# A decoder layer on one core: the lower-threshold compare of the feed-forward weights moves from VectorE to GpSimd

## The chip, the core and the metric

The kernel runs on one core of a Trainium2 chip. Its five engines (TensorE, VectorE, ScalarE, GpSimd and SyncE, which here only issues DMAs) each work through their own list of instructions in order and meet through semaphores. The profile calls them PE (with PEld for weight loads), DVE, ACT, POOL and SP. The metric is the device time of one execution in microseconds; the kernel before takes 1132.5 us (median of 3 runs, 1131.54 to 1132.69).

## The reference

One decoder layer over x of shape (4, 512, 512), float32, in three parts, each with a residual:

```
x = x + attention(layernorm(x))                        # 16 heads, rotary, causal
x = x + ssm(ctx, gate = layernorm(x))                  # convolution, selective scan over 16 states, silu gate
x = x + bitlinear(gelu(bitlinear(layernorm(x), w_fc)), w_proj)

def ternarize_weights(w):
    gamma = jnp.mean(jnp.abs(w))
    return jnp.sign(jnp.round(w / (gamma + EPS))) * gamma
```

Both feed-forward matrices (2048 x 512 and 512 x 2048) are made ternary before use: a weight above half of gamma becomes +1, one below minus half becomes -1, all others 0. This is (w > thr) - (w < -thr) with thr = (gamma + 1e-6) / 2, and gamma is multiplied in later.

## The kernel before, in words

The four batches are worked through as a pipeline in which attention, the state-space scan and the feed-forward tiles of different batches overlap. The work is cut into named items. A planner (`plan()`) walks a table of due times (`schedule()`, with the constants of `WEIGHT`), the needs and assumed durations of each item (`follows()`), and writes one ordered list per engine, `ORDER["pe"]`, `ORDER["act"]`, `ORDER["dve"]`, `ORDER["pool"]`, `ORDER["sp"]`. It also decides the PSUM bank of each item, and how many dummy transposes (L1599) TensorE does while it stands by. The program of an engine is its list, item by item.

The items that matter here, with the lines of the profile:

- `dbu` (GpSimd, L1263) makes the scan's inputs in the ring `hb`; `exp` (ScalarE, L1394) makes its factors in PSUM; `scan` (VectorE, L1812, in the tail L1820) runs over `hb`; `ht` (TensorE L1725, VectorE L1834) turns the states and adds them up in `y_acc`. The factors of one scan are made only when the scan before it is through. In the last batch a piece is half as long (128x512).
- `s`, `e`, `t`, `pv`, `rz` are attention: row maxima on VectorE (L1905, L1909), exponentials on ScalarE (L1505), transposes, the product with v, the reciprocal of the sums (L1917). `wo` (TensorE L1737, VectorE L1932) is the output projection. `ln2a`, `ln2b` are the norm in front of the gate: statistics on VectorE, one power on GpSimd (L1317), one small operation on VectorE (L1947). `gate` is a silu on ScalarE (L1536), `gt` its product (VectorE L1956), `xadd` the residual on GpSimd (L1306).
- `fwload`, `wsum`, `wtot`, `tern` treat the feed-forward weights, matrix `w` = 0 (`raw_fc`) and 1 (`raw_pr`), in four parts of 128x2048 each: load, sum of absolute values on ScalarE (L1576, it writes its unused output to `low`), total over partitions and the thresholds `thr` and `nthr` on VectorE (L1963 to L1968), and then the ternary values.
- `tern` in the kernel before is two VectorE instructions for each part: L1977 writes `low` = (w < nthr) in bf16, L1979 writes (w > thr) - low over the same weights, in the form that TensorE reads (`t_fc`, `t_pr`). There is one `low` buffer, shared by all parts and by `wsum`. The semaphore `tern_done` counts both instructions.
- `xa`, `xc`, `xt`, `fc`, `hstat`, `hn`, `hscale`, `hq`, `ht_ffn`, `proj` are the 16 feed-forward tiles. `xc` is a subtraction and a maximum on VectorE (L2004, L2006), then a scaling on GpSimd (L1340).

Of the kernel before, what the change touches and what calls it, by code (L numbers as in the profile page):

```python
# [437 lines left out]
def follows(item):  # L438
# [157 lines left out]
        yield "dve", 1.2, [pe(*item)]  # L596
    elif kind == "tern":
        w, n = a
        yield "dve", 3.7, [dve("wtot", w)]
    elif kind == "fxload":  # L600
        t, = a
        yield "sp", 1.6, [sp("x2store", *divmod(t, LT)), dve("proj", t - XF) if t >= XF else pe("pv", SLOTS // 2 - 1)]
# [187 lines left out]
def layer_kernel(nc, t_in, out):  # L790
    sems = {}
    with ExitStack() as ctx:
# [185 lines left out]
        fw_in = [[sem(f"fw_in{w}{c}") for c in range(4)] for w in range(2)]  # L978
        wsum_ready = sem("wsum_ready")
        gam_ready = sem("gam_ready")  # L980
        tern_done = sem("tern_done")
        xf_in = [sem(f"xf_in{i}") for i in range(XF)]
        fx_var = sem("fx_var")
# [258 lines left out]
        def _(pool):  # L1242
# [11 lines left out]
            for kind, *a in ORDER["pool"]:  # L1254
# [64 lines left out]
                elif kind == "xa":  # L1319
# [12 lines left out]
                    own.done(nc.gpsimd.tensor_tensor(f[:, 3:4], f[:, 5:6], neg_half[:, 0:1], ALU.pow))  # L1332
                    own.settle()
                    nc.gpsimd.tensor_scalar(f[:, 7:8], f[:, 2:3], f[:, 3:4], None, ALU.mult).then_inc(fx_gain, 1)
                elif kind == "xc":

                    t, = a
# [27 lines left out]
        def _(act):  # L1365
# [7 lines left out]
            for kind, *a in ORDER["act"]:  # L1373
# [182 lines left out]
                elif kind == "fc":  # L1556
                    t, n = a
                    act.wait_ge(fc_full, 4 * t + n + 1)
                    act.wait_ge(fx_scale, t + 1)
                    if t >= 2:  # L1560
                        act.wait_ge(tr_full, TURN["ht_ffn", t - 2, 3] + 1)
                    elif t == 1:
                        act.wait_ge(xadd_done, LT * (B - 1))
                    nc.scalar.activation(h_sb[:, t % 2, 512 * n:512 * n + 512], bank(kind, t, n), ACT.Gelu,
                                         scale=fx[:, t % 4, 12:13]).then_inc(gelu_done, 1)
                elif kind == "wsum":

                    w, n = a
                    c = PARTS[w][n]
                    act.wait_ge(fw_in[w][c], 16)  # L1570
                    i = 4 * w + n
                    if i:
                        act.wait_ge(wsum_ready, i)
                    if w:
                        act.wait_ge(tern_done, 8)
                    nc.scalar.activation(low[:], raw[w][:, c, :], ACT.Abs, accum_out=w_sum[:, w, c:c + 1])\  # L1576
                        .then_inc(wsum_ready, 1)
                elif kind == "hn":

                    t, h = a  # L1580
                    act.wait_ge(fh_var, t + 1)
                    half = h_sb[:, t % 2, FF // 2 * h:FF // 2 * (h + 1)]
                    nc.scalar.activation(half, half, ACT.Identity, bias=fh[:, t % 4, 0:1], scale=-1.0).then_inc(hn_done, 1)
# [3 lines left out]
        def _(pe):  # L1587
# [13 lines left out]
            for kind, *a in ORDER["pe"]:  # L1601
# [174 lines left out]
                elif kind == "fc":  # L1776

                    t, n = a
                    pe.wait_ge(tr_free, TURN["xt", t] + 1)
                    pe.wait_ge(tern_done, 8)  # L1780
                    for d in range(KD):
                        for m, part in enumerate((xq_hi, xq_lo)):
                            mm = nc.tensor.matmul(bank(kind, t, n), part[:, t % 2, d, :], t_fc[:, d, 512 * n:512 * n + 512],  # L1783
# [1 line left out]
                    mm.then_inc(fc_full, 1)  # L1785
                elif kind == "proj":
                    t, = a
                    pe.wait_ge(tern_done, 16)
                    pe.wait_ge(tr_free, TURN["ht_ffn", t, 3] + 1)
                    for k in range(FT):  # L1790
                        for m, part in enumerate((hq_hi, hq_lo)):
# [6 lines left out]
        def _(dve):  # L1798
# [5 lines left out]
            for kind, *a in ORDER["dve"]:  # L1804
# [153 lines left out]
                elif kind == "wtot":  # L1958
# [6 lines left out]
                    v.tensor_scalar(g, g, 1.0 / (DM * FF), None, ALU.mult).then_inc(gam_ready, 1)  # L1965
                    dve.wait_ge(gam_ready, w + 1)
                    own.done(v.tensor_scalar(thr[:, w:w + 1], g, EPS_Q, 0.5, ALU.add, ALU.mult))
                    own.done(v.tensor_scalar(nthr[:, w:w + 1], g, EPS_Q, -0.5, ALU.add, ALU.mult))  # L1968
                    own.settle()
                elif kind == "tern":  # L1970

                    w, n = a
                    c, n = PARTS[w][n], 4 * w + n
                    dst = (t_fc[:, c, :], t_pr[:, 4 * c:4 * c + 4, :].rearrange("p a n -> p (a n)"))[w]
                    if n:
                        dve.wait_ge(tern_done, 2 * n)
                    v.tensor_scalar(low[:], raw[w][:, c, :], nthr[:, w:w + 1], None, ALU.is_lt).then_inc(tern_done, 1)  # L1977
                    dve.wait_ge(tern_done, 2 * n + 1)
                    v.scalar_tensor_tensor(out=dst, in0=raw[w][:, c, :], scalar=thr[:, w:w + 1], in1=low[:],  # L1979
                                           op0=ALU.is_gt, op1=ALU.subtract).then_inc(tern_done, 1)  # L1980
                elif kind == "xa":
# [147 lines left out]
```

## Time and profile before

| | |
|---|---|
| median of 3 runs | 1132.5 us (1131.54 to 1132.69) |
| the profiled execution | 1132.71 us, its span 1130.8 us |
| TensorE busy | 1003.4 us (89%) |
| VectorE busy | 958.6 us (85%) |
| ScalarE busy | 794.0 us (70%) |
| GpSimd busy | 630.2 us (56%) |
| mean granted TensorE clock | 0.961 of full speed |

The span runs from the first instruction to the last one that the profiler recorded; 1.9 us of the execution lie around it. Busy time is the time in which an engine had an instruction under way. As the stages have different limits, what a change in one of them is worth is read from that stretch of the span.

### The profile page before, as it was taken

Reading aid. Unit: us, or ns where it says so; the run is one execution under the profiler, and the core shown is the slowest. Engines: PE = TensorE matmul, PEld = TensorE weight load, DVE = VectorE, ACT = ScalarE, POOL = GpSimd, SP = SyncE. Lnnn points to the kernel's source line nnn. Section 1 sums busy time; section 2 is a strip of 40 time slices with the busy share of each in tenths; the row PEclk is TensorE's granted clock in tenths of the full one; section 3 lists DMA queues with packets and bytes.
Section 4 is the critical chain, followed back from the end, with each engine's and each line's share of the span. In section 5 each row is a group of like instructions: output and inputs, shape, how many; then the busy total and the mean of one; then the engine's idle time right before and its main releaser. Section 6 shows DMA issues by size and latency. Waiting matters only on the chain.

```text
span 1130.8 us, 19021 instructions
## 1 busy us (share of the span) xinstructions
PE 1003.4 (89%) x6054; PEld 762.8 (67%) x6054; DVE 958.6 (85%) x1351; ACT 794.0 (70%) x1533; POOL 630.2 (56%) x509
## 2 busy tenths in 40 slices
PE   6988998899988999898999986797788987999998
PEld 5555776566855567765558765676676776778887
DVE  5788679778698987988996889989999999998764
ACT  4854866667588776489867688955989888874342
POOL 1458468346336787526657853467766565653510
PEclk9999998999998999999999988799899999999999
DMA  4324546256445354333366371340111010100000
GB/s 158 113 85 140 160 136 184 64 150 196 129 117 152 128 162 145 127 115 112 112 186 190 106 237 50 110 171 10 52 38 37 30 52 29 24 15 20 19 19 19
DMA packets 59360, 115.91 MB, mean 103 GB/s; under 512 B 8880, under 2 KB 13232, under 8 KB 58240
## 3 DMA queue, kind: packets, MB, share of 16 engines
q1 hardware_dynamic: 59264, 114.70, 32.7%
q8 instruction: 51, 0.84, 0.3%
q14 instruction: 45, 0.37, 0.1%
HBM read 90.42 MB, written 24.25 MB: 101 GB/s over the span
## 4 chain that ended last, share of the span: by engine, by line
PE 54%; DVE 23%; issue 10%; ACT 8%; POOL 3%; DMA 1%; SPq 0%; DVEq 0%; ACTq 0%; POOLq 0%
PE ps L1656 8%; PE ps L1792 7%; PE ps L1725 7%; DVE hb L1812 6%; PE ps L1783 5%; PE ps L1737 5%; PE ps L1669 5%; PE ps L1699 4%; DVE y_acc L1834 4%; PE ps L1711 3%; DVE hb L1820 2%; PE ps L1680 2%; PE ps L1599 2%; DVE m_col L1909 2%; PE ps L1774 2%
## 5 line engine op out<-in xcount | busy, mean ns | idle before, releaser
L1263 POOL TENSOR_TENSOR hb<-du,b_bc 128x1024 f32<-128x1024 f32 (+1 forms) x160 | 312.1, 1972 | 147.0 <-PE ps L1725 141.6
L1812 DVE TENSOR_TENSOR_SCAN hb<-ps,hb 128x1024 f32<-128x1024 f32 (+1 forms) x128 | 257.6, 2014 | 21.7 <-ACT ps L1394 12.3
L1394 ACT ACTIVATE ps<-delta,a_neg 128x511 f32<-128x511 f32 (+2 forms) x320 | 180.5, 600 | 93.3 <-DVE hb L1812 78.9
L1834 DVE SCALAR_TENSOR_TENSOR y_acc<-ps,ct,y_acc 128x512 f32<-128x512 f32 x256 | 180.9, 740 | 29.7 <-PE ps L1725 29.0
L1725 PE MATMUL ps<-ident,hb 128*128 128x128 f32 x1088 | 155.4, 286 | 55.6 <-DVE hb L1812 28.6
L1725 PEld LDWEIGHTS ps<-ident,hb 128*128 128x128 f32 x1088 | 127.5, 146 | 87.3 <-issue 36.9
L1505 ACT ACTIVATE p_q<-ps,m_col 128x512 f32<-128x512 f32 (+3 forms) x256 | 131.5, 533 | 15.7 <-DVE m_col L1909 14.0
L1656 PE MATMUL ps<-xn_t,w_ring 128*128 128x512 f32 x256 | 118.3, 605 | 2.9 <-DVE hl L1890 2.9
L1699 PE MATMUL ps<-ident,p_q 128*128 128x128 f32 x640 | 93.9, 296 | 18.0 <-ACT p_q L1505 12.6
L1783 PE MATMUL ps<-t_fc,xq_hi 128*128 128x512 f32 x256 | 106.4, 415 | 2.6 <-DVE hq_lo L2026 1.2
L1521 ACT ACTIVATE p_t<-ps 128x512 f32<-128x512 f32 x160 | 86.0, 604 | 27.0 <-PE ps L1699 26.7
L1792 PE MATMUL ps<-t_pr,hq_hi 128*128 128x512 f32 x256 | 101.5, 396 | 0.6 <-DVE hq_lo L2026 0.6
L1783 PE MATMUL ps<-t_fc,xq_lo 128*128 128x512 f32 x256 | 102.0, 398 | 0.0
L1792 PE MATMUL ps<-t_pr,hq_lo 128*128 128x512 f32 x256 | 101.1, 395 | 0.0
L1699 PEld LDWEIGHTS ps<-ident,p_q 128*128 128x128 f32 x640 | 78.7, 152 | 32.5 <-ACT p_q L1505 17.3
L1909 DVE TENSOR_REDUCE m_col<-ps 128x1 f32<-128x512 f32 (+2 forms) x192 | 88.0, 501 | 10.6 <-PE ps L1684 8.0
L1656 PEld LDWEIGHTS ps<-xn_t,w_ring 128*128 128x128 f32 x256 | 47.4, 194 | 55.2 <-issue 49.6
L1680 PE MATMUL ps<-k_st,q_st 128*128 128x512 f32 (+3 forms) x256 | 74.8, 372 | 11.1 <-DVE y_acc L1834 6.1
L1599 PE MATMUL ps<-ident 128*128 128x128 f32 x498 | 68.6, 288 | 8.7 <-DMA small<-in_small 6.2
L1294 POOL TENSOR_TENSOR hl<-hl 128x512 f32<-128x512 f32 x16 | 20.4, 1274 | 97.7 <-DVE hl L1897 97.7
L1599 PEld LDWEIGHTS ps<-ident 128*128 128x128 f32 x498 | 60.4, 149 | 14.0 <-DMA small<-in_small 6.2
L1375 ACT ACT_TABLE_LOAD x47 | 60.3, 1283 | 0.8
(159 smaller groups left out, 2016.6 us busy)
## 6 DMA issues: line engine op xcount, KB each, us to landing
w_ring<-in_w_attn SPq DMA_DIRECT2D x32, 512.0 KB, 3.6
qk_d<-hl SPq DMA_DIRECT2D x64, 256.0 KB
q_st<-qk_d SPq DMA_DIRECT2D x128, 128.0 KB, 2.8
b_bc<-bc_d SPq DMA_DIRECT2D x48, 256.0 KB, 3.7
k_st<-qk_d SPq DMA_DIRECT2D x64, 128.0 KB, 2.7
k_st<-qk_d SPq DMA_DIRECT2D x128, 64.0 KB, 2.3
x_in<-in_x SPq DMA_DIRECT2D x16, 256.0 KB, 2.8
raw_fc<-in_w_fc SPq DMA_DIRECT2D x4, 1024.0 KB, 8.5
```

What stands on the lines that cost most here:

```text
L1263: nc.gpsimd.tensor_tensor(piece_of(e, hi, lo).rearrange("p (a n) -> p a n", a=2), du[b % 2][:, 2 * h:2 * h + 2, lo:hi], b_bc[:, i % BC_RIN ...
L1394: ins = nc.scalar.activation(factors(j, hi, lo)[:, (hi - lo) * m + start:(hi - lo) * (m + 1)], delta[b % 2][:, et, lo + start:hi], ACT.Exp ...
L1505: ins = nc.scalar.activation(p_q[:, h, Q_AT[i]:Q_AT[i] + w], src[:, col:col + w], ACT.Exp, bias=m_col[:, i, h:h + 1], accum_out=z_sum[:, b ...
L1599: nc.tensor.transpose(bank(*item)[:, 0:P], ident[:], ident[:])
L1656: mm = nc.tensor.matmul(bank(kind, *a), w_ring[:, c % 2, d, P * half:P * half + P], xn_t[:, d, :], start=(d == 0), stop=(d == KD - 1))
L1699: mm = nc.tensor.transpose(dst[:, at:at + P], p_q[:, h, Q_AT[i] + P * jt:Q_AT[i] + P * jt + P], ident[:])
L1725: mm = nc.tensor.transpose(bank(kind, *a)[:, P * et:P * et + P], piece_of(2 * r + et // 2, hi, lo)[:, at:at + P], ident[:])
L1783: mm = nc.tensor.matmul(bank(kind, t, n), part[:, t % 2, d, :], t_fc[:, d, 512 * n:512 * n + 512], start=(d == 0 and m == 0), stop=(d == K ...
L1792: mm = nc.tensor.matmul(bank(kind, t), part[:, k, :], t_pr[:, k, :], start=(k == 0 and m == 0), stop=(k == FT - 1 and m == 1))
L1812: v.tensor_tensor_scan(h, d, h, 0.0, ALU.mult, ALU.add).then_inc(scan_done, 1)
L1834: v.scalar_tensor_tensor(out=y, in0=bank(kind, r, tb), scalar=ct[:, b % 2, tb, n:n + 1], in1=y, op0=ALU.mult, op1=ALU.add).then_inc(y_free ...
L1909: ins = v.tensor_reduce(m_col[:, i, h:h + 1], src[:, col:col + P * (i + 1)], AX.X, ALU.max, negate=True)
```

## The change

The first instruction of `tern` moves from VectorE to GpSimd. A new semaphore `thr_ready` tells GpSimd that the thresholds of a matrix stand, `low_ready` tells VectorE that a part's compare is through, and `tern_done` now counts only VectorE's instruction, so that all waits on it halve. GpSimd's compare of a part waits for VectorE's combination of the part before, since there is one `low`. The planner is told of a GpSimd share of 4.7 and a VectorE share of 2.5 in place of one VectorE share of 3.7.

```diff
     elif kind == "tern":
         w, n = a
-        yield "dve", 3.7, [dve("wtot", w)]
+        yield "pool", 4.7, [dve("wtot", w)] + ([dve("tern", *divmod(4 * w + n - 1, 4))] if w or n else [])
+        yield "dve", 2.5, [pool(*item)]
...
+                elif kind == "tern":
+
+                    w, n = a
+                    c, n = PARTS[w][n], 4 * w + n
+                    pool.wait_ge(thr_ready, w + 1)
+                    if n:
+                        pool.wait_ge(tern_done, n)
+                    nc.gpsimd.tensor_scalar(low[:], raw[w][:, c, :], nthr[:, w:w + 1], None, ALU.is_lt).then_inc(low_ready, 1)
...
                     if w:
-                        act.wait_ge(tern_done, 8)
+                        act.wait_ge(tern_done, 4)
...
                     own.done(v.tensor_scalar(thr[:, w:w + 1], g, EPS_Q, 0.5, ALU.add, ALU.mult))
-                    own.done(v.tensor_scalar(nthr[:, w:w + 1], g, EPS_Q, -0.5, ALU.add, ALU.mult))
+                    v.tensor_scalar(nthr[:, w:w + 1], g, EPS_Q, -0.5, ALU.add, ALU.mult).then_inc(thr_ready, 1)
...
-                    if n:
-                        dve.wait_ge(tern_done, 2 * n)
-                    v.tensor_scalar(low[:], raw[w][:, c, :], nthr[:, w:w + 1], None, ALU.is_lt).then_inc(tern_done, 1)
-                    dve.wait_ge(tern_done, 2 * n + 1)
+                    dve.wait_ge(low_ready, n + 1)
                     v.scalar_tensor_tensor(out=dst, in0=raw[w][:, c, :], scalar=thr[:, w:w + 1], in1=low[:],
                                            op0=ALU.is_gt, op1=ALU.subtract).then_inc(tern_done, 1)
```

Since the planner reads these shares, the lists of all engines differ from the first feed-forward total on (the `wtot` of matrix 0, near 682 us of the trace); ahead of it they are the same. In the lists the lines of the changed kernel are 3 to 11 higher on GpSimd and VectorE. ScalarE's list holds 97 table loads in place of 100.

GpSimd around the parts of matrix 0 (`hb` are the scan's inputs, `du` those of the next batch). Before:

```order
L1263 TENSOR_TENSOR hb<-du_98,b_bc 128x1024 x11
L1288 TENSOR_TENSOR du_95<-delta_96,du_95 128x512 x4
L1263 TENSOR_TENSOR hb<-du_95,b_bc 128x512 x8
```

After:

```order
L1266 TENSOR_TENSOR hb<-du_98,b_bc 128x1024 x5
L1345 TENSOR_SCALAR low<-raw_fc,nthr 128x2048
L1266 TENSOR_TENSOR hb<-du_98,b_bc 128x1024 x2
L1345 TENSOR_SCALAR low<-raw_fc,nthr 128x2048 x2
L1266 TENSOR_TENSOR hb<-du_98,b_bc 128x1024 x2
L1345 TENSOR_SCALAR low<-raw_fc,nthr 128x2048
L1266 TENSOR_TENSOR hb<-du_98,b_bc 128x1024 x2
```

The first compare stands ahead of the pair of scan inputs for which GpSimd was free before, and the second and third stand together ahead of the next pair.

VectorE in the same place (`gam`, `thr`, `nthr` are the total and the thresholds, the 128x1024 operations on `hb` the scans). Before:

```order
L1968 TENSOR_SCALAR nthr<-gam 128x1
L1977 TENSOR_SCALAR low<-raw_fc,nthr 128x2048
L1979 SCALAR_TENSOR_TENSOR t_fc<-raw_fc,thr,low 128x2048
L1812 SCALAR_TENSOR_TENSOR hb<-ps,hb 128x1024
L1834 SCALAR_TENSOR_TENSOR y_acc<-ps,ct,y_acc 128x512
L1917 RECIPROCAL z_sum<-z_sum 128x16
```

After:

```order
L1979 TENSOR_SCALAR nthr<-gam 128x1
L1845 SCALAR_TENSOR_TENSOR y_acc<-ps,ct,y_acc 128x512
L1823 SCALAR_TENSOR_TENSOR hb<-ps,hb 128x1024
L1928 RECIPROCAL z_sum<-z_sum 128x16
L1823 SCALAR_TENSOR_TENSOR hb<-ps,hb 128x1024
L1987 SCALAR_TENSOR_TENSOR t_fc<-raw_fc,thr,low 128x2048
```

Two scans now stand ahead of the first combination.

GpSimd behind the output projection `wo`, with the third and fourth compare of matrix 1 (`xq` is the scaling of a feed-forward tile, `rstd_72` the power that the norm in front of the gate waits for, `xr` the residual). Before:

```order
L1340 TENSOR_SCALAR xq<-xq,fx 128x512
L1345 TENSOR_SCALAR fx<-fx,gam 128x1
L1317 TENSOR_TENSOR rstd_72<-ve_71,neg_half 128x4
```

After:

```order
L1351 TENSOR_SCALAR xq<-xq,fx 128x512
L1356 TENSOR_SCALAR fx<-fx,gam 128x1
L1266 TENSOR_TENSOR hb<-du_95,b_bc 128x512
L1345 TENSOR_SCALAR low<-raw_pr,nthr 128x2048
L1320 TENSOR_TENSOR rstd_72<-ve_71,neg_half 128x4
L1309 TENSOR_TENSOR xr<-xr,y_acc 128x512 x4
L1345 TENSOR_SCALAR low<-raw_pr,nthr 128x2048
```

The power now stands behind a scan input and a compare.

## Rows read from the trace of the kernel before

**Rows 1.** The page, part 4: the chain by engine, share of the span.

```profile
PE 54%; DVE 23%; issue 10%; ACT 8%; POOL 3%; DMA 1%; SPq 0%; DVEq 0%; ACTq 0%; POOLq 0%
```

**Rows 2.** Windows: stretch, length, busy us (count) per engine, PE clock, DMA share, GB/s.

```profile
680.00:700.00 20.00, 13.30 (x124) 9.66 (x122) 19.82 (x20) 16.60 (x31) 5.70 (x2) 0.83 0.18 56
700.00:720.00 20.00, 13.38 (x73) 10.67 (x74) 19.73 (x23) 18.59 (x37) 6.73 (x3) 0.78 0.02 7
...
780.00:800.00 20.00, 13.65 (x78) 11.48 (x76) 19.78 (x23) 19.73 (x25) 16.02 (x13) 0.91 0.03 8
...
980.00:1000.00 20.00, 17.58 (x90) 14.21 (x88) 19.79 (x34) 15.54 (x23) 12.50 (x17) 1.00 0.14 33
...
1020.00:1040.00 20.00, 20.00 (x109) 16.86 (x107) 18.42 (x32) 7.65 (x12) 7.11 (x12) 1.00 0.07 27
```

**Rows 3.** Timeline of VectorE, matrix 0: start, duration, instruction, idle time before it.

```profile
682.60 2.48 DVE L1977 TENSOR_SCALAR low<-raw_fc,nthr 128x2048 bf16<-128x2048 f32 x1
685.11 4.36 DVE L1979 SCALAR_TENSOR_TENSOR t_fc<-raw_fc,thr,low 128x2048 fp32r<-128x2048 f32 x1
689.39 2.28 DVE L1812 TENSOR_TENSOR_SCAN hb<-ps,hb 128x1024 f32<-128x1024 f32 x1
...
692.39 1.19 DVE L1977 TENSOR_SCALAR low<-raw_fc,nthr 128x2048 bf16<-128x2048 f32 x1
693.62 2.35 DVE L1979 SCALAR_TENSOR_TENSOR t_fc<-raw_fc,thr,low 128x2048 fp32r<-128x2048 f32 x1
...
724.45 1.28 DVE L1977 TENSOR_SCALAR low<-raw_fc,nthr 128x2048 bf16<-128x2048 f32 x1
```

**Rows 4.** Timeline of GpSimd beside it.

```profile
681.62 5.70 POOL L1263 TENSOR_TENSOR hb<-du,b_bc 128x1024 f32<-128x1024 f32 x2 [2.77 <-PE ps L1725]
704.33 4.69 POOL L1263 TENSOR_TENSOR hb<-du,b_bc 128x1024 f32<-128x1024 f32 x2 [17.01 <-PE ps L1725]
```

**Rows 5.** Lines by form: line, engine, operation, count, busy us, mean ns, idle before.

```profile
L1263 POOL TENSOR_TENSOR hb<-du,b_bc 128x512 f32<-128x512 f32 x64 | 85.4, 1357 | 30.7 <-PE ps L1725 30.7
...
L1340 POOL TENSOR_SCALAR xq<-xq,fx 128x512 f32<-128x512 f32 x16 | 32.4, 2026 | 12.8 <-DVE fx L2008 11.9
...
L1251 POOL TENSOR_SCALAR_AFFINE_SELECT ident_r<-xn_t 128x128 fp32r<-128x128 f32 x1 | 0.3, 292 | 0.3 <-POOL xn_t L1248 0.3
...
L1246 POOL MEMSET neg_half<- 128x4 f32 x1 | 0.1, 101 | 0.0
```

**Rows 6.** Timeline of ScalarE: factors of a scan, a sum of weights; the page's table loads.

```profile
691.78 1.30 ACT L1394 ACTIVATE ps<-delta,a_neg 128x511 f32<-128x511 f32 x2 [1.58 <-DVE hb L1812]
732.57 1.91 ACT L1576 ACTIVATE low<-raw_pr 128x2048 bf16<-128x2048 f32 x1
...
L1375 ACT ACT_TABLE_LOAD x47 | 60.3, 1283 | 0.8
```

**Rows 7.** Timeline of TensorE: the output projection.

```profile
755.86 13.98 PE L1737 MATMUL ps<-w_ring,o_t 128*128 128x256 f32 x64
```

**Rows 8.** Timeline of VectorE, matrix 1.

```profile
758.17 1.27 DVE L1977 TENSOR_SCALAR low<-raw_pr,nthr 128x2048 bf16<-128x2048 f32 x1
...
767.73 2.33 DVE L1812 TENSOR_TENSOR_SCAN hb<-ps,hb 128x512 f32<-128x512 f32 x2
...
779.48 0.16 DVE L1947 SCALAR_TENSOR_TENSOR nmr<-mv,rstd 128x4 f32<-128x4 f32 x1 [0.41 <-POOL rstd L1317]
...
782.44 0.67 DVE L1990 BATCH_NORM_STATS2 st_x<-xf 128x6 f32<-128x512 f32 x1
...
783.24 1.26 DVE L1977 TENSOR_SCALAR low<-raw_pr,nthr 128x2048 bf16<-128x2048 f32 x1
...
786.80 0.68 DVE L1956 TENSOR_TENSOR y_acc<-ps,y_acc 128x512 f32<-128x512 f32 x1
...
791.10 1.47 DVE L1977 TENSOR_SCALAR low<-raw_pr,nthr 128x2048 bf16<-128x2048 f32 x1
```

**Rows 9.** Timeline of GpSimd behind the output projection.

```profile
778.41 1.04 POOL L1317 TENSOR_TENSOR rstd<-ve,neg_half 128x4 f32<-128x4 f32 x1
```

More of the change, by code:

```diff
@@ L980, in layer_kernel @@
         gam_ready = sem("gam_ready")
+        thr_ready = sem("thr_ready")
+        low_ready = sem("low_ready")
         tern_done = sem("tern_done")
@@ L1779, in _ @@
                     pe.wait_ge(tr_free, TURN["xt", t] + 1)
-                    pe.wait_ge(tern_done, 8)
+                    pe.wait_ge(tern_done, 4)
                     for d in range(KD):
@@ L1787, in _ @@
                     t, = a
-                    pe.wait_ge(tern_done, 16)
+                    pe.wait_ge(tern_done, 8)
                     pe.wait_ge(tr_free, TURN["ht_ffn", t, 3] + 1)
```

## The prediction, made before the changed kernel ran

> **What bounds the kernel now.** I read the page first, then the windows of the span, then the timelines of VectorE and GpSimd around the ternary conversion. The page gives TensorE 54% of the chain, VectorE 23% [rows 1]; that is an average, and the conversion lies in a stretch that looks otherwise. From 680 to 720 us VectorE is busy 19.8 and 19.7 of 20 us, TensorE only 13.3 and 13.4, GpSimd 5.7 and 6.7 [rows 2]: VectorE sets the pace, and GpSimd has time. From 756 to 770 us TensorE runs the output projection without a gap, 13.98 us [rows 7], and VectorE's work beside it costs nothing. From 780 us VectorE is full again (19.78 of 20, still 19.79 at 980 to 1000), and from 1020 us TensorE is (20.00 of 20) [rows 2], up to the end. So a microsecond taken from VectorE at 680 to 728 us or behind 780 us should come out at the end, and one taken at 756 to 770 us should not.
>
> **The price of the compare on GpSimd.** The trace has no one-operation compare of this engine, so I bound it. A select over 128 columns took 292 ns, a fill of 4 columns 101 ns [rows 5]: less such a start it is 1.5 ns a column, which for 2048 columns makes 3.2 us. A two-input multiply took 4.69 us for two of 1024 columns, so 4.7 us for 2048 [rows 4]. A tensor_scalar with two operations took 2026 ns for 512 columns, so up to 8.1 us for 2048 [rows 5]. The compare does one operation on one input. I take 4.0 us, the middle of the two one-operation rows, and keep 3.2 and 8.1 as ends. The page "GPSIMD Engine Reference" of the Trainium skill, section "Engine selection", says that one-input operations run at roughly line rate; at its 1.2 GHz that is an estimate of 1.7 us, below my lower end, and by it the sum would be that of the first rival. No row here shows such a rate: the two-operation row is far above it.
>
> **Stretch 1, matrix 0 (682 to 728 us).** Four compares leave VectorE: 2.48, 1.19 and, for the third like the fourth, 1.28, together 6.2 us [rows 3]. What comes back:
> - The second scan behind the thresholds now stands ahead of the first combination. Its factors are made only after the first scan, 1.30 us [rows 6], a gap that the second compare and combination filled before. VectorE has only the reciprocal for it: +1.3.
> - A combination that meets a GpSimd multiply is stretched: 4.36 us beside the pair at 681.62, 2.35 alone [rows 3, 4], 2.0 more. The first combination meets a pair in both kernels. The third is new in this: GpSimd starts the next pair as soon as its third compare is through. Bounds 0 and 2.0; I take +1.0.
> - The waits for `low_ready`. GpSimd runs the first compare from 682.6 to 686.6; VectorE comes to the combination at about 689.3 (682.5 and an operation of 0.7, two scans of 2.2 [rows 3], 1.5 between them). The combination of 4.36 ends at 693.7 and releases the second compare, to 697.7; VectorE has a scan and four operations of 0.65 first, to 698.4. The third runs from 700.9 to 704.9, VectorE has a scan and seven small operations, to about 707.4. So no wait at 4.0 us; from 4.7 us on it begins. The scan inputs that are pushed back (from 681.6 to 686.6) still land before their scan at 694.
> Sum -3.9 us.
>
> **Stretch 2 (728 to 756 us).** ScalarE's second sum of matrix 1, 1.91 us and its readout [rows 6], moves from a place where ScalarE had time to one between scan factors, ahead of the total that stands before the output projection. Bounds 0 and 2.1; I take +1.0. The projection begins 2.9 us earlier.
>
> **Stretch 3 (756 to 770 us).** Two compares leave VectorE (the first 1.27 us [rows 8], the second like it), both beside the projection [rows 7]: 0. GpSimd's two compares must fit there with VectorE's combinations between them: 756 + 4.0 + 2.35, a little VectorE work, then 4.0 + 2.35 again ends at about 769, with the projection's end at 769.8. From a compare of 4.4 us on this decides, and each further microsecond costs two.
>
> **Stretch 4 (770 to 800 us).** Two compares leave VectorE: 1.26 + 1.47 = -2.7 [rows 8]. By the new order two scans (2.33 us) come from ahead of the projection's end to behind it, +2.3, and two gate products (0.68 each) and a statistics step (0.67) go the other way into covered time, -2.0 [rows 8]. The power for the norm stands behind a scan input and a compare: GpSimd is through with the second scaling at about 778.4 [rows 9], then about 1.3 (a scan input, from the 1357 ns of [rows 5]) + 4.0 + 1.04 give 784.7, where VectorE comes to it at about 782.2; before, it waited 0.41 [rows 8]. In VectorE's list the scans and everything else queue behind that small instruction, and ScalarE's factors and TensorE's turns behind the scans: +2.5. The fourth compare waits for the residual additions and ends at 793.7, VectorE is there at 792.9: +0.8. The third combination meets the residual additions, which read two inputs: bounds 0 and 2.0, +1.0. Sum +1.9 us.
>
> **Behind 800 us** the same work stands in another order on a full VectorE and then a full TensorE: 0. ScalarE's list holds three table loads less, 1.28 us each [rows 6], 3.8 us; they lie beside the full VectorE, so I count 0 and keep 3.8 for the better end.
>
> **Sum.** -3.9 + 1.0 + 0 + 1.9 = -1.0 us. The profiled execution took 1132.71 us (span 1130.8 and 1.9 around it), which is the median of the runs, 1132.5, within 0.02%. 1132.7 - 1.0 = 1131.7 us. That is inside 0.2% (2.3 us), about what a measurement of this kernel can tell from no change.
>
> **On the port.** Rows show a combination of 4.36 us against 2.35, and VectorE's compare of 2.48 against about 1.28, each beside the same GpSimd pair, which itself took 5.70 in place of 4.69 [rows 3, 4]. The page "SBUF — State Buffer" of the Trainium skill, section "Who interferes with whom", says why: a VectorE instruction with two SBUF inputs, or in a mode that takes both ports, shares a port pair with GpSimd, and whoever starts second is held for the whole instruction of the other. The trace agrees with a hold of one instruction. That rule speaks against the change, since it puts eight long GpSimd reads beside VectorE; what it gives is the third rival.
>
> **Rivals.**
> 1. *The saving comes through.* The compare takes 3.2 us and no combination meets a multiply. Then stretch 1 gives -4.9, stretch 2 nothing, stretch 4 -2.7 + 2.3 - 2.0 + 1.7 = -0.7: -5.6 us, 1127.1 us, and down to 1123.3 if the table loads count too. For it: GpSimd stands idle 17.01 us in front of one pair [rows 4]. Against: the norm's power is behind a compare whatever it costs.
> 2. *The compare takes the two-operation rate (slower).* At 7.6 us, a little under the 8.1 of [rows 5], VectorE waits for `low` 1.0, 3.1 and 0.9 us in stretch 1, +5.0. In stretch 3 both compares and combinations end at 776.2 in place of 770: +6.2, on the way of the first feed-forward tile, because VectorE's last drain of the projection stands behind the second combination. In stretch 4 the power and the fourth compare come 3.6 us later each, +7.2. Together 18.4 more than the forecast: 1150.1 us. It decides from about 4.7 us on. For it: the only long tensor_scalar of GpSimd has this rate. Against: that one does two operations.
> 3. *VectorE is held (slower).* The compare is short, but the fourth stands beside VectorE's subtraction for the third tile, which is of the kind that was stretched from 1.28 to 2.48, and is held up to 4.0 us, with up to 1.0 more for the third combination. That makes 1134.7 to 1136.7 (3.0 to 5.0 more), say 1135.7 us. Against: it takes an overlap that depends on a microsecond.
> That the change does nothing can be left out: the compares leave VectorE for certain.
>
> **How the numbers follow.** Chances: forecast 0.32 (of it 0.26 within 0.2%, 0.04 faster, 0.02 slower), rival 1 0.31 (0.29 faster, 0.02 within), rival 2 0.21 (all slower), rival 3 0.16 (0.13 slower, 0.03 within). That makes faster 0.33, within 0.31, slower 0.36. The likeliest is the forecast, 1131.7 us; its own range by the bounds of the two collisions and of the sum's move is 1128.7 to 1134.8. As cases of both signs hold much of the chance, the whole range is 1125 to 1147, which leaves out the far end of rival 1 and something over half of rival 2.
>
> **What would show it.** GpSimd's compare in the profile after: 3 to 5 us bears the forecast or rival 1, 7 to 8 us rival 2. VectorE's combination at 2.35 us in all but two or three of eight; four or more near 4.4 us, or a VectorE tensor_scalar of 128x512 above 2 us, bear rival 3. The small norm operation should wait for the power some 2.5 us, the first combinations not at all for `low`. The projection should begin near 753 us. If the compare is short and VectorE has no new waits, yet the end comes late, then the order behind 800 us, which I counted as nothing, was not nothing, and the prediction is wrong there.

## The result and the profile after

The changed kernel takes 1151.37 us (median of 4 runs, 1147.39 to 1153.46), the kernel before 1132.60 us beside it: ratio 1.0162, 95% interval [1.0147, 1.0177], so 18.4 us slower. The forecast was 1131.7 us with a range up to 1147. The profiled execution took 1153.46 us (span 1151.7). Left out of every figure below are three executions of over 3300 us (3376.56 in e1, 3336.59 in e4, 4696.50 in e7; in the two that were profiled TensorE was busy for the whole span), so that e1 was profiled once more, as e1b.

The page, part 4, of the changed kernel, against [rows 1]:

```profile
PE 48%; DVE 21%; issue 12%; ACT 10%; POOL 8%; DMA 1%; SPq 0%; DVEq 0%; ACTq 0%; POOLq 0%
```

GpSimd's share of the chain went from 3% to 8%: it is now waited for. The groups of GpSimd's instructions on `low` (count, shortest, median and longest in ns, first and last start):

```profile
L1345 POOL TENSOR_SCALAR low<-raw_fc,nthr x4: 5432/5437/5457, 682.9 to 715.2; 128x2048 bf16<-128x2048 f32 x4
L1345 POOL TENSOR_SCALAR low<-raw_pr,nthr x4: 5443/5456/5462, 755.4 to 800.6; 128x2048 bf16<-128x2048 f32 x4
```

A compare is 5.44 us where I had taken 4.0 (and where the estimate of 1.7 us that the prediction sets beside it is three times too short). The windows, against [rows 2], columns as there:

```profile
680.00:700.00 20.00, 13.46 (x115) 10.08 (x117) 16.09 (x17) 18.76 (x36) 17.05 (x4) 0.83 0.18 55
700.00:720.00 20.00, 15.11 (x103) 11.06 (x95) 18.41 (x19) 10.85 (x26) 17.45 (x5) 0.82 0.12 32
780.00:800.00 20.00, 12.80 (x64) 10.61 (x64) 13.84 (x15) 5.84 (x11) 17.05 (x11) 0.84 0.17 60
...
1020.00:1040.00 20.00, 17.25 (x90) 14.17 (x91) 19.79 (x34) 16.25 (x24) 11.09 (x17) 1.00 0.00 1
```

At 780 to 800 us VectorE is busy 13.84 us where it was 19.78: it stands still there, in the stretch in which it had set the pace. VectorE's timeline of the changed kernel at matrix 0, against [rows 3]:

```profile
689.42 3.47 DVE L1987 SCALAR_TENSOR_TENSOR t_fc<-raw_fc,thr,low 128x2048 fp32r<-128x2048 f32 x1
...
700.55 2.35 DVE L1987 SCALAR_TENSOR_TENSOR t_fc<-raw_fc,thr,low 128x2048 fp32r<-128x2048 f32 x1 [2.14 <-POOL low L1345]
```

GpSimd's and then VectorE's timeline at matrix 1, against [rows 8, 9]:

```profile
755.43 5.46 POOL L1345 TENSOR_SCALAR low<-raw_pr,nthr 128x2048 bf16<-128x2048 f32 x1
760.87 0.22 POOL L1327 TENSOR_SCALAR fx<-fx 128x1 f32<-128x1 f32 x1
761.17 2.53 POOL L1329 TENSOR_TENSOR fx<-fx,neg_half 128x1 f32<-128x1 f32 x1
...
765.47 5.46 POOL L1345 TENSOR_SCALAR low<-raw_pr,nthr 128x2048 bf16<-128x2048 f32 x1
...
785.65 5.45 POOL L1345 TENSOR_SCALAR low<-raw_pr,nthr 128x2048 bf16<-128x2048 f32 x1
791.06 1.04 POOL L1320 TENSOR_TENSOR rstd<-ve,neg_half 128x4 f32<-128x4 f32 x1
792.07 4.99 POOL L1309 TENSOR_TENSOR xr<-xr,y_acc 128x512 f32<-128x512 f32 x4
800.62 5.44 POOL L1345 TENSOR_SCALAR low<-raw_pr,nthr 128x2048 bf16<-128x2048 f32 x1 [3.57 <-DVE t_pr L1987]
```

```profile
760.93 2.35 DVE L1987 SCALAR_TENSOR_TENSOR t_pr<-raw_pr,thr,low 128x2048 fp32r<-128x2048 f32 x1 [1.72 <-POOL low L1345]
...
770.97 3.35 DVE L1987 SCALAR_TENSOR_TENSOR t_pr<-raw_pr,thr,low 128x2048 fp32r<-128x2048 f32 x1 [4.86 <-POOL low L1345]
774.24 0.68 DVE L1943 TENSOR_TENSOR xr_last<-ps,xr_last 128x512 f32<-128x512 f32 x1
...
792.14 4.93 DVE L1958 SCALAR_TENSOR_TENSOR nmr<-mv,rstd 128x4 f32<-128x4 f32 x1 [4.20 <-POOL rstd L1320]
...
801.03 5.31 DVE L2012 TENSOR_SCALAR xq<-xf,fx 128x512 f32<-128x512 f32 x1
```

VectorE comes to the second combination 4.86 us too early, and the last drain of the projection (774.24) stands behind it. It waits 4.20 us for the norm's power. The small product `nmr`, 0.16 us before, takes 4.93 us: it starts as GpSimd's four residual additions do and ends with them. In this text an instruction that starts beside one of GpSimd's, lasts much longer than elsewhere and ends just behind it is called held. A 128x512 subtraction, 0.48 us before, takes 5.31: it ends 0.28 us behind the fourth compare. TensorE's timeline, against [rows 7]:

```profile
754.79 13.98 PE L1748 MATMUL ps<-w_ring,o_t 128*128 128x256 f32 x64
781.89 1.11 PE L1785 MATMUL ps<-ident,xq 128*128 128x128 f32 x4 [9.85 <-POOL xq L1351]
808.55 1.94 PE L1736 MATMUL ps<-ident,hb 128*128 128x128 f32 x8 [13.53 <-DVE hb L1823]
```

TensorE waits 9.85 us in front of tile 0's first transposes, and later 13.53 us for the scan that stands behind the held subtraction on VectorE.

Five marks place the loss. The first is the first feed-forward total on VectorE (681.97 before), up to which every kernel here runs the same instructions; then the start of the projection (755.86), tile 0's first transposes (775.88), tile 0's hidden statistics on VectorE (801.39, the aggregate of 128x24) and the span (1130.8). In us against before, from one profiled execution each:

| kernel | first total | projection | transposes | statistics | span |
|---|---|---|---|---|---|
| changed | +0.3 | -1.1 | +6.0 | +16.4 | +20.9 |
| e1b: its lists, all work on VectorE | +1.5 | +2.4 | +2.9 | +5.9 | +9.6 |
| e2: only matrix 0 on GpSimd | +1.6 | -0.8 | -0.3 | +2.7 | +6.1 |
| e3: only matrix 1 on GpSimd | -2.0 | -1.1 | +6.0 | +12.5 | +16.1 |
| e10: e1, tail of before | -3.1 | -1.0 | -0.4 | +2.3 | +4.7 |
| e16: e1, lists of matrix 0 alone | +0.1 | +0.3 | +0.3 | +0.3 | +1.9 |
| e17: e1, lists of matrix 1 alone | -0.7 | -0.6 | +0.9 | +6.4 | +9.2 |
| e18: e1, three items put back | +1.4 | +4.3 | +6.4 | +10.3 | +13.1 |
| e14: compares half as long | +1.0 | -4.8 | -2.7 | -1.3 | +2.1 |
| e12: matrix 0 alone, planned so | -0.5 | -3.1 | -3.1 | -3.3 | -0.8 |
| e19: e12 and 22 empty matmuls | -0.6 | -3.2 | -3.2 | -3.4 | -2.4 |

What stands under "first total" is the execution's own and no work of the change, and has to be taken off the other columns: e1b and e10, alike up to tile 0's statistics, come to it 4.5 us apart, and once it is taken off they differ by 1.2 us at the projection and 1.0 at the statistics. One execution is no median even so (that of e3 lies 6 us under the median of its runs). The marks show where, and the medians and ratios below show how much.

### The profile page after: what moved, and what is told of

Read it like the earlier page. It is cut to its first block, busy times and chain, and to the rows that moved or that the text cites. A ratio compares the mean times of both kernels' runs of the same rounds, so it can differ in the third digit from the quotient of the medians.

```text
span 1151.7 us, 18999 instructions
## 1 busy us (share of the span) xinstructions
PE 1002.3 (87%) x6042; PEld 758.2 (66%) x6042; DVE 957.7 (83%) x1343; ACT 789.6 (69%) x1530; POOL 671.9 (58%) x517
## 4 chain that ended last, share of the span: by engine, by line
PE 48%; DVE 21%; issue 12%; ACT 10%; POOL 8%; DMA 1%; SPq 0%; DVEq 0%; ACTq 0%; POOLq 0%
PE ps L1667 8%; PE ps L1803 7%; PE ps L1736 6%; PE ps L1680 5%; DVE hb L1823 5%; PE ps L1710 4%; PE ps L1794 4%; PE ps L1748 3%; POOL hb L1266 3%; DVE y_acc L1845 3%; PE ps L1722 2%; ACT ps L1405 2%; DVE hb L1831 2%; DVE m_col L1920 2%; PE ps L1691 2%
## 5 line engine op out<-in xcount | busy, mean ns | idle before, releaser
L1266 POOL TENSOR_TENSOR hb<-du,b_bc 128x1024 f32<-128x1024 f32 (+1 forms) x160 | 316.2, 1994 | 124.6 <-PE ps L1736 119.5
L1736 PE MATMUL ps<-ident,hb 128*128 128x128 f32 x1088 | 158.4, 289 | 71.1 <-DVE hb L1823 41.9
L1691 PE MATMUL ps<-k_st,q_st 128*128 128x512 f32 (+3 forms) x256 | 72.6, 363 | 13.1 <-DVE y_acc L1845 7.6
L1610 PE MATMUL ps<-ident 128*128 128x128 f32 x486 | 66.2, 284 | 8.1 <-DMA small<-in_small 5.6
L1610 PEld LDWEIGHTS ps<-ident 128*128 128x128 f32 x486 | 57.5, 147 | 13.2 <-DMA small<-in_small 5.6
L1575 ACT ACTIVATE h_sb<-ps,fx 128x512 f32<-128x512 f32 x64 | 43.0, 685 | 26.8 <-PE ps L1794 26.4
```

What stands on the lines that cost most here:

```text
L1266: nc.gpsimd.tensor_tensor(piece_of(e, hi, lo).rearrange("p (a n) -> p a n", a=2), du[b % 2][:, 2 * h:2 * h + 2, lo:hi], b_bc[:, i % BC_RIN ...
L1610: nc.tensor.transpose(bank(*item)[:, 0:P], ident[:], ident[:])
L1736: mm = nc.tensor.transpose(bank(kind, *a)[:, P * et:P * et + P], piece_of(2 * r + et // 2, hi, lo)[:, at:at + P], ident[:])
```

## The experiments

Theory A: the loss is the length of the compares at matrix 1 and what they hold up. Rival B: the new lists lose by themselves.

**Lists, and each matrix apart.** e1 keeps the lists of the change, but VectorE does both instructions; e2 and e3 leave one matrix on GpSimd.

```diff
+ON_POOL = ()                     # e1; (0,) in e2, (1,) in e3
...
 GpSimd:   elif kind == "tern":
+    if w not in ON_POOL: continue
...
 VectorE:  elif kind == "tern":
+    if w not in ON_POOL:
+        v.tensor_scalar(low[:], raw[w][:, c, :], nthr[:, w:w + 1], None, ALU.is_lt).then_inc(low_ready, 1)
```

> All lists of the changed kernel, but VectorE does both instructions of every part, one after the other, and GpSimd none. Theory A (the price is GpSimd's compare of 5.44 us and what it blocks): about the time before, 1130 to 1138 us, since VectorE gets its 10 us of compares back and loses its waits. Rival B (the new order of the lists is what costs): at least 1145 us.

> Lists of the changed kernel, GpSimd compares matrix 0 only, VectorE does both instructions for matrix 1. Theory A: matrix 0 waited only 2.1 us for the compare in the changed kernel and had its compares of 6 us removed, so this is 1 to 4 us faster than the kernel with the same lists and no compare on GpSimd. Rival B: as that kernel, at least 1145 us.

> Lists of the changed kernel, GpSimd compares matrix 1 only. Theory A: nearly the whole loss is here (waits of 1.7 and 4.9 us for the compare, 4.2 for the norm's power, 4.8 and 4.8 us in which VectorE's small norm operation and its subtraction were held): 1146 to 1154 us. Rival B: as the kernel with the same lists and no compare on GpSimd, within 2 us.

Measured: e1 1140.10 us, ratio 1.0061 [1.0044, 1.0078], between what A and what B gave; e2 1138.40, 1.0041 [1.0026, 1.0055]; e3 1154.60, 1.0178 [1.0149, 1.0206]. With the changed kernel that is a square of two by two. By the ratios the lists cost 7 us with no work moved, GpSimd's compares of matrix 0 give 2 us back (inside the intervals) and those of matrix 1 cost 13. The three add up to the whole. A is right for matrix 1, B for the rest; my forecast had neither. VectorE's timeline of e3, where the changed kernel had 4.93 and 5.31:

```profile
792.15 1.24 DVE L1961 SCALAR_TENSOR_TENSOR nmr<-mv,rstd 128x4 f32<-128x4 f32 x1 [4.22 <-POOL rstd L1321]
...
797.35 0.82 DVE L2020 TENSOR_SCALAR xq<-xf,fx 128x512 f32<-128x512 f32 x1
...
804.74 3.34 DVE L1995 SCALAR_TENSOR_TENSOR t_pr<-raw_pr,thr,low 128x2048 fp32r<-128x2048 f32 x1 [3.27 <-POOL low L1348]
```

The long holds that A counted on are not there, and still this execution loses 13.6 us between projection and statistics, against 17.5 in the changed kernel. Of VectorE's waits it has one more, 3.27 us for the fourth compare. So the waits carry most of the loss at matrix 1, and the long holds some 4 us of it in the executions that have them.

**The lists of before.** e4 keeps them and only inserts the eight compares into GpSimd's list.

```diff
+ORDER["pool"].insert(ORDER["pool"].index(after) + 1, ("tern", w, n))
```

> Lists of the kernel before on all engines; GpSimd's eight compares are put into its list where it had time: two behind the scan inputs 91, one each behind 93 and 95, behind the first feed-forward scale of the second tile, behind 105, behind the norm's power, and behind the third tile's scaling. VectorE has only the combinations. Theory A: the norm's power comes in time, so it is cheaper than the changed kernel, but the compares of matrix 1 still do not fit beside the output projection and still hold VectorE: 1134 to 1146 us. Rival B: the removed compares come through, 1122 to 1130 us.

Measured: 1163.71 us, 1.0271 [1.0254, 1.0288], slower than either theory had it. VectorE's waits from 660 to 860 us (in total, times, longest):

```profile
DVE t_pr L1992 <- POOL low L1350: 21.3, 4, 7.1
DVE t_fc L1992 <- POOL low L1350: 19.2, 4, 9.3
```

All eight combinations wait. With the compares at these places in the lists of before, the kernel is 12 us slower by the ratios than with the new lists, which themselves cost 7 against before. Other places were not tried.

**What the holds cost.** e6 writes `nmr` as four one-input instructions of 128x1, e7 puts the norm's power ahead of GpSimd's third compare.

```diff
-v.scalar_tensor_tensor(out=nmr, ...)                 # 128x4, two inputs
+for i in range(4): v.tensor_scalar(nmr[:, i:i + 1], ...)
...
+_p.insert(_p.index(("tern", 1, 2)), ("ln2a", B - 1))     # e7, GpSimd's list
```

> The changed kernel, with one edit: the small norm operation on VectorE, one instruction of 128x4 with two tensors from SBUF that lasted 4.93 us beside four residual additions of GpSimd, is written as four of 128x1, each with one tensor and scalars. Theory D (it was held at the port by its second tensor): none of the four lasts over 0.3 us, and the kernel gains 2 to 5 us, 1146 to 1150 us. Rival (the record shows something else, a late semaphore or GpSimd's own load): they end as late as before and the time stays at 1151 us.

> The changed kernel, with the norm's power of the last batch put ahead of GpSimd's third compare of matrix 1. Theory A: VectorE's wait of 4.2 us for it goes, and the compare ends 1.0 us later; 3 to 6 us faster, 1145 to 1149 us. Rival (what is taken here comes back as a wait for the third or fourth compare, since VectorE comes to them earlier): less than 1.5 us.

Measured: e6 1148.19 us, 1.0132 [1.0115, 1.0149], 3.4 us better by the ratios than the change. VectorE's timeline of e6:

```profile
790.37 0.58 DVE L1959 TENSOR_SCALAR nmr<-mv,rstd 128x1 f32<-128x1 f32 x4 [4.22 <-POOL rstd L1320]
790.86 1.21 DVE L1823 TENSOR_TENSOR_SCAN hb<-ps,hb 128x512 f32<-128x512 f32 x1
791.99 5.44 DVE L1988 SCALAR_TENSOR_TENSOR t_pr<-raw_pr,thr,low 128x2048 fp32r<-128x2048 f32 x1
```

`nmr` is free, the scan too, and now the third combination, 2.32 us in the change, is held until the additions (790.29 to 795.29 here) are through and ends 2.1 us behind them. So the hold moved on to the next two-input instruction. e7: 1150.20 us, 1.0156 [1.0139, 1.0173]: no gain from putting the power first. That what it frees is waited for later was the rival's reading; the profile of e7 is of an execution of 4696.50 us and doesn't show it.

**The length.** e14 compares 1024 of the 2048 columns.

```diff
-nc.gpsimd.tensor_scalar(low[:], raw[w][:, c, :], nthr[...], None, ALU.is_lt)
+nc.gpsimd.tensor_scalar(low[:, :1024], raw[w][:, c, :1024], nthr[...], None, ALU.is_lt)
```

> The change with each GpSimd compare over 1024 of the 2048 columns; the other half of `low` is left as it stood, so half of the thresholding is not computed. The compare should take 2.7 to 2.8 us if its time goes by columns (5.44 at 2048). Theory A (13 us of the loss is the length of the compares at matrix 1, above all the two ahead of tile 0's transposes, plus the holds): with half the length 1139 to 1143 us, near e1's 1141.0, and less the 2.6 us of matrix 0 perhaps 1137. Rival H (the loss is the handover between the engines and VectorE's holds, not the length): above 1146 us.

Measured: 1134.73 us, 1.0014 [1.0001, 1.0027]. Groups of e14:

```profile
L1345 POOL TENSOR_SCALAR low<-raw_fc,nthr x4: 2843/2846/2867, 683.6 to 712.2; 128x1024 bf16<-128x1024 f32 x4
L1345 POOL TENSOR_SCALAR low<-raw_pr,nthr x4: 2848/2862/2862, 751.7 to 788.0; 128x1024 bf16<-128x1024 f32 x4
```

2.6 us less per compare brings 16.8 us (1.0162 less 1.0014, times 1132.6) of the 18.4 back. Lists and handovers are the same: what the change pays for hangs on the length, and rival H falls as a cost of its own. The waits go with it: VectorE waits 1.69 us for the norm's power and 0.71 in all for `low` of matrix 1, and in this profile `nmr` takes 1.24 us and the subtraction 0.85. It is 4 us under A's range, and 5 faster than e1 with the same lists. So the 7 us of the lists are their price with the work as it is in e1, and are no fixed charge.

**The planner's price.** e8 tells the planner 5.5 for a compare; e15 does half of each compare on either engine, all of it computed, with 2.8 and 3.1.

```diff
-yield "pool", 4.7, ...
+yield "pool", 5.5, ...          # e8; in e15 2.8, and VectorE 3.1 in place of 2.5
...
+v.tensor_scalar(low[:, 1024:], raw[w][:, c, 1024:], nthr[...], None, ALU.is_lt)   # e15, VectorE
```

> The change with one number altered: the planner counts 5.5 us for a compare on GpSimd in place of 4.7. The third compare of matrix 0 then stands one scan-input product later, and the tail is ordered anew. Theory A (the compare's real length costs 13 us at matrix 1, wherever the list puts it, since nothing can be moved under it): 1146 to 1152 us. Rival G (the planner merely had the wrong price and with the right one avoids the waits): 1133 to 1142 us.

> A version that the results point to: of each part GpSimd compares columns 0 to 1023 and VectorE columns 1024 to 2047 (0.63 us), then VectorE combines all 2048; the planner counts 2.8 us and 3.1 us. Everything is computed. By e14 a half compare takes GpSimd 2.7 us and is in time for VectorE. If the length was what cost the change its 18 us, and the lists do no harm, the four us that VectorE is spared show in part: 1128 to 1132 us. If an order made for new costs loses by itself as in e1: 1134 to 1141 us.

Measured: e8 1148.79 us, 1.0136 [1.0120, 1.0152]; e15 1138.20 us, 1.0036 [1.0022, 1.0050]. The right price saves 3 us (the two intervals touch) and not the change, as A said. The halves are slower than before too, as the second case had it: its tile 0 transposes wait 8.07 us for GpSimd's scaling, 2.99 before.

**Which lists.** e16 and e17 take the lists of one matrix each, with all work on VectorE. e1b is the profile of e1.

```diff
 elif kind == "tern":
+    if w in PLANNED:            # (0,) in e12, e16, e19; (1,) in e17
         yield "pool", ...       # 5.5 in e12, e16, e19; 4.7 in e17
         yield "dve", 2.5, ...
+    else:
+        yield "dve", 3.7, [dve("wtot", w)]
```

> The lists of e12 (only matrix 0 planned on GpSimd), but VectorE does both instructions of all eight parts and GpSimd none. Theory I (the new order around matrix 0 costs nothing, and GpSimd's compares give the little that e12 has): 1132 to 1134 us, and tile 0's statistics at 801 to 802 us. Rival J (this order by itself costs 2 to 3 us, which e12's compares pay for; the lists' loss of e1 lies partly here): 1135 to 1137 us.

> Only matrix 1 is planned on GpSimd (at 4.7 us, as in the change), and VectorE does both instructions of all eight parts. Theory K (the lists' 8 us of e1 lie in matrix 1's part and the tail that it reorders): 1138 to 1142 us. Rival J (they lie in matrix 0's part): 1132 to 1135 us.

> e1 once more for its profile. From e2 and e10: tile 0's statistics on VectorE (801.39 us before) at 804 to 806 us, the end 6 to 8 us late. If the lists' loss lies ahead (theory E): the statistics 5 us late or more; if behind (theory D): under 3 us late and 5 us lost after that.

Measured: e16 1134.10 us, 1.0002 [0.9991, 1.0012]; e17 1142.38, 1.0075 [1.0061, 1.0089]; e1b 1142.21 (one run). The lists' loss is matrix 1's alone. By the marks of e17, 7 us of it fall between the start of the projection and tile 0's statistics and 3 behind; by those of e1b, less its 1.5 at the first total, 0.9 ahead of the projection, 3.5 there and 3.7 behind.

**What in them.** e5 puts GpSimd's scalings of tiles 4 to 9 ahead of the scan's operands in e1. e10 follows the change's lists up to tile 0's statistics and those of before from there. e18 puts back matrix 1's total and scans 104 and 105.

```diff
 e10: lists[engine] = head of the change + [x for x in before[engine] if x not in head]
 e18: move("pe", [("wtot", 1)], ahead of ("ht", 54, 0)); move("dve", [("wtot", 1)], ahead of ("xa", 0))
      move("dve", [("scan", 104), ("scan", 105)], ahead of ("wo", 3, 1, 1))
```

> As the kernel with the changed lists and both instructions on VectorE (1141.0 us), but in GpSimd's list the scaling of the feed-forward tiles 4 to 9 stands ahead of the one, two or three scan inputs that the new order put before it, as in the kernel before. Theory C (the lists cost their 8 us because TensorE waits for that scaling, 9.0 us in five waits from 832 to 1004 us in the kernel with matrix 0 on GpSimd, none before): 4 to 7 us faster, 1134 to 1137 us. Rival (the 8 us are spread over the order of VectorE and ScalarE): less than 2 us, 1139 us or more.

> The lists of e1 again, with both instructions of every part on VectorE, but spliced: each engine follows the lists of the changed kernel up to tile 0's statistics (VectorE's `hstat` 0, near 815 us) and the lists of the kernel before from there on; banks and empty matmuls are worked out anew for the spliced lists. e1 lost 8.1 us to the lists. Theory D (the loss lies in the order behind 815 us, in tiles 0 to 9, as the starts of the output tiles suggest: 1.9 us early at tile 0 in e2, 6.1 us late at the end): with the tail of the kernel before nearly all comes back, 1131 to 1135 us. Rival E (the head lists leave the engines in a state, by what was pulled ahead or put off, from which the tail is late whatever its order): 1139 to 1142 us, as e1.

> e1 (lists of the change, all work on VectorE) with three items put back where the kernel before has them: the weight sum of matrix 1 ahead of the conversion statistics of tile 0 on VectorE and ahead of state turn 54 on TensorE, and scans 104 and 105 ahead of the last projection copy, so ahead of tile 0's first transposes. Theory L (tile 0's chain is late because VectorE, which has no idle time there, does this work first): 2.3 to 5 us come back, 1136 to 1139.5 us, and tile 0's statistics stand 2 to 5 us earlier than in e1b_look. Rival M (the place of these items does not matter, the loss is spread over many small swaps): 1140 to 1143 us.

Measured: e5 1145.13 us, 1.0105 [1.0090, 1.0120], 5 us worse than e1 by the ratios; the same edit on e2 (e9) gave 1141.42, 1.0075 [1.0059, 1.0091], 4 us worse. e10 1138.98, 1.0049 [1.0035, 1.0064]: 1.4 us better than e1, inside the intervals. e18 1142.47, 1.0085 [1.0069, 1.0102]: not better. Theories C (the scaling's place), D (the tail's order) and L (these three items) all fall as the main cause. Which swap in the lists of matrix 1 costs the 7 to 8.5 us stays open. For the stretch between projection and statistics the profiles show by what it comes. VectorE's timeline of e1b:

```profile
762.56 2.05 DVE L1993 TENSOR_SCALAR low<-raw_pr,nthr 128x2048 bf16<-128x2048 f32 x1
764.65 3.23 DVE L1995 SCALAR_TENSOR_TENSOR t_pr<-raw_pr,thr,low 128x2048 fp32r<-128x2048 f32 x1
...
798.19 3.26 DVE L1995 SCALAR_TENSOR_TENSOR t_pr<-raw_pr,thr,low 128x2048 fp32r<-128x2048 f32 x1
```

Before, these take 1.28, 2.35 and 2.35 us. Here each meets a scan-input multiply of GpSimd that is already under way; before, the multiplies beside the two combinations start 0.09 and 0.14 us behind them, and it is GpSimd that takes longer. In this stretch VectorE does the same work in both kernels. What its instructions last beyond the median of their form in the kernel before adds up to 5.2 us in e1b and to 0.2 before, and it is idle 1.3 us less: together 3.7 us, where the marks give 3.5. In e17 the two terms are +5.2 and +2.0 for 7.0 us (`nmr` alone waits 3.41 and takes 3.73 us), in e18 +7.4 and -0.5 for 6.0. This is read from one execution each and was not put to the test. The 3 to 4 us behind the statistics stay open.

**A version that is not slower.** e12 plans and runs matrix 0 alone on GpSimd; VectorE's list in it is that of before from 767 us of the trace on, not from 740 as the text below has it: a gate product and a few other items around the projection stand elsewhere. e19 adds empty matmuls ahead of one state turn.

```diff
+FILLS["ht", 60, 0] += 22        # e19
```

> The planner is told of matrix 0 alone that GpSimd compares (at 5.5 us, what the compare takes), and of matrix 1 that VectorE does both (3.7 us); the kernel does so. The lists differ from those before only up to the first output projections (near 740 us) and are the same word for word behind. Theory D: the 2.6 to 3.2 us that matrix 0 gave in e2 are kept and nothing is lost behind: 1129 to 1131 us, faster than before. Rival E (what the lists lost, they lost ahead of 800 us): 1136 to 1140 us, as e2. Rival F (matrix 0's gain is absorbed by what is late next, the gate transposes and matrix 1): 1132 to 1134 us.

> e12 with 22 empty matmuls ahead of state turn 60 on TensorE, where it stood idle for 3.0 us at 814 us before the granted clock fell to 0.56 and 0.58 in 816 to 824 us (1.00 in the kernel before). Theory N (the half clock takes what tile 0 had won): the clock stays at 1.00 there and the end comes 1 to 2 us earlier than e12's, 1130 to 1131 us. Rival O (the end is set by VectorE, which hardly notices the clock): no difference, 1131.5 to 1132.5 us. If the empty matmuls stand in the way of the scans' inputs instead: 1133 us or more.

Measured: e12 1132.09 us, 0.9992 [0.9981, 1.0003]; e19 1130.86 us, 0.9985 [0.9975, 0.9994]. e12 is what rival F gave, e19 what theory N gave. Windows of e12, of e19:

```profile
808.00:816.00 8.00, 6.27 (x32) 4.91 (x30) 7.79 (x15) 7.43 (x12) 3.91 (x7) 1.00 0.00 2
816.00:824.00 8.00, 6.73 (x23) 5.87 (x24) 7.84 (x11) 7.05 (x13) 6.06 (x8) 0.57 0.10 30
```

```profile
808.00:816.00 8.00, 8.00 (x50) 6.95 (x49) 7.79 (x15) 7.42 (x13) 4.07 (x7) 1.00 0.02 4
816.00:824.00 8.00, 6.66 (x40) 5.37 (x39) 8.00 (x11) 7.20 (x12) 6.30 (x8) 1.00 0.19 32
```

Counted from the first total, e12 is 2.8 us early at tile 0's statistics and 0.3 at the end. In it TensorE stood idle 3.0 us up to 817.27, and in the 8 us from 816 on the granted clock averages 0.57, near its lower level (1.2 in place of 2.4 GHz). The kernel before has 1.00 there, but 0.79 in the 8 us ahead of it. With the gap filled the clock stays at 1.00 in both stretches, and this execution is 1.8 us early at the end. By the ratios the empty matmuls are worth 0.8 us, inside the intervals of the two. e19 beats the kernel before by 1.7 us [0.7, 2.8], less than the 0.2% I had called measurable, though the interval excludes no change; the changed kernel it beats by 20.

## Why the prediction was wrong

*The price.* "I take 4.0 us": it is 5.44, between my ends. I averaged a start-corrected select and a two-input multiply. The nearest row by kind, the tensor_scalar [rows 5], would have missed by more the other way (8.1), so no row gave the price; the multiply (4.7) and the tensor_scalar hold it between them. By the two lengths, 5.44 and 2.85 us, a column costs 2.5 ns and the start 0.3 us. The trace before had none of this, but my text had the point from which the price decides, 4.4 to 4.7 us, only just above my value: a forecast so near its own threshold should have leaned to the other side of it.

*Stretch 1, -3.9.* Measured -1.4 at the projection, counted from the first total, where stretches 1 and 2 together were to give -2.9. The second combination waits 2.14 us for `low`, which I had at nothing and rival 2 at 3.1. The first combination met the pair as in the forecast, but takes 3.47 in place of 4.36; the collision of the third, +1.0, did not come (2.34). The sign held, and e2 and e12, with the same compares, come to -2.4 and -2.6: these two stretches were nearly right.

*Stretch 3, 0.* This is the step that failed most, that both compares fit beside the projection and cost nothing: +7.1 between projection and transposes, where rival 2 had +6.2 from a compare of 7.6. I had called VectorE's work there covered by the projection, and both were full: before, VectorE is busy 13.89 of the 14.00 us from 756 to 770, so that nothing longer than what left could pass unseen. I had placed the second compare right behind the first combination. In GpSimd's list tile 1's six factor instructions stand between them, 760.87 to 765.47, one of them a 0.56 us power that VectorE's combination stretches to 2.53. So the mechanism of rival 2 decided at a price of 5.44 already.

*Stretch 4, +1.9.* Measured +10.4 (from +6.0 to +16.4). The wait for the power was foreseen at 2.5 and is 4.2. The hold of the subtraction was rival 3's ("held up to 4.0"), and came to 4.83 us more than its own time. That of `nmr`, 4.77 us more, was in no case: I had looked for one of the third combination there (+1.0), which at 2.32 us was not held. I had read the port from one pair of instructions as a hold of one instruction. The page "SBUF — State Buffer" of the Trainium skill, section "Who interferes with whom", says that the one that comes first has the shared ports for its whole instruction while the other is blocked. The first combination agrees: it starts at 689.42 beside the first multiply of a pair and ends 2.15 us behind that one, and the pair takes 6.73 in place of 4.69 us, since the second multiply waits in its turn. `nmr` was held over four additions, so the measurement goes further. e6 shows that avoiding one hold moves it to the next candidate, and e3 that the loss is mostly there without the long ones.

*Behind 800 us, 0.* Wrong, as the last sentence of the prediction allowed for. The changed kernel loses 4.5 us behind tile 0's statistics. The lists cost 7 us with no work moved (e1) and 8.5 with matrix 1's alone (e17). More than half of that is ahead of 800 us, where I had priced the moved instructions one by one at +0.3 (+2.3 - 2.0) and not whom they would meet on GpSimd. In the square the terms are: lists +7 (forecast near 0), matrix 0's compares -2, matrix 1's +13 (forecast near 0).

*Rival 2* was the right mechanism with a chance of 0.21 and a time of 1150.1 us, 1.3 from the result. That nearness is luck in part: it had the compare 2 us too long and held the lists at nothing.

## What to carry to other kernels

Work is given to an idle engine only if each piece is short against the slack at its place, not against the engine's idle share: half the length took away 16.8 of 18.4 us lost, and the same work at a place with slack (matrix 0) gave 1 to 2 us by the ratios, each time inside the intervals. Price an unseen instruction by a range between the nearest rows on either side, and when the threshold lies within that range, let the forecast follow the worse side. Compare profiles from the last point up to which the kernels do the same, not from the start. Where a planner orders everything, run its new lists without the moved work first: that separates the cost of the order from that of the work (here 7 against 13 us, less the 2 that matrix 0 gives back).

## What was not expected of the hardware

- GpSimd's one-operation compare of 128x2048 f32 into bf16 takes 5.43 to 5.47 us, and 2.84 to 2.87 for 1024 columns. It hardly varies beside other work.
- A two-input VectorE instruction can be held over a whole run of back-to-back GpSimd two-input instructions: 4.93 us for a 128x4 product beside four additions of 4.99. It need not be: with the same start beside the same additions the product took 1.24 us in e3, to the end of the first. What decides between the two, no run here shows. In e18 a combination of 2.35 took 5.89 beside three scan-input multiplies:

```profile
799.97 3.77 POOL L1284 TENSOR_TENSOR hb<-du,b_bc 128x512 f32<-128x512 f32 x3
```

```profile
799.99 5.89 DVE L2012 SCALAR_TENSOR_TENSOR t_pr<-raw_pr,thr,low 128x2048 fp32r<-128x2048 f32 x1
```

- VectorE's one-input 128x512 subtraction is held beside GpSimd's compare (5.31 in place of 0.48 us), while a scan of 1.21 us and one-input 128x1 instructions run beside GpSimd's additions unheld (e6). It also goes the other way: a 128x1 power of GpSimd took 2.53 us in place of 0.56 beside a combination.
- With the same instructions up to there, executions come to the first total up to 4.7 us apart (678.89 us in e10, 683.61 in e2).
